# The third half projection of the next head, moved in front of the decay products

## The chip, the cores and the metric

The kernel runs on one core of a Trainium2 chip. The metric is the time of one execution on the device, in microseconds (us). A profiled execution is one further run, from which all rows of the trace below come; it has its own time.

## The reference, cut to what matters

All arithmetic is 32-bit floating point. The program is a chain of a gated delta-rule attention layer with 32 value heads, a perceptron, a second attention layer and a mixture of experts. The change lies in the first of these, with 1024 tokens of width 256:

```python
mixed = hidden_states @ w_qkv                      # 256 -> 2048 q, 2048 k, 4096 v
mixed = jax.nn.silu(_causal_conv(mixed, conv_w))   # 4 taps over the tokens
...
def step(state, xs):
    q_t, k_t, v_t, g_t, b_t = xs
    state = state * jnp.exp(g_t)[..., None, None]
    kv = jnp.einsum('bhk,bhkv->bhv', k_t, state)
    delta = (v_t - kv) * b_t[..., None]
    state = state + jnp.einsum('bhk,bhv->bhkv', k_t, delta)
    out = jnp.einsum('bhk,bhkv->bhv', q_t, state)
    return (state, out)
```

## The kernel before

The 16 key heads (each with two value heads) are worked one after the other, the tokens in 8 chunks of 128. The recurrence is replaced by a chunked form. A step h of the loop `STEPS` works on four heads at once: it projects the inputs of head h + 1 (`AHEAD`, steps 0 to 14), inverts the chunk matrices of head h (`INVERT`, steps 0 to 15), scans the state of head h - 1 through the chunks (`SCAN`, steps 1 to 16) and writes the output of head h - 2 (`FINISH`, steps 2 to 17).

Every engine runs through the same list of rows: `QUANTA` has 23 parts of the scan (chunk c, part 0, 1 or 2), and behind the part k an engine does what row k of `PLAN` names. A name stands for a group of products on PE and for what other engines do with their result. So `PLAN` is an order written out by hand, for PE, VectorE and ScalarE at once. The number beside a name is the PSUM bank, 0 to 3, into which the group is written. Per bank there are semaphores `full` and `free`, whose values are counted from the order in `PLAN`; a group waits until the one before it in its bank has been evacuated.

The names around the change:

- p0 to p7 (L531, `project`): the projections of the next head. Tensor j (key, query, two values) is made by p(2j) and p(2j+1), one half of the tokens each, as two products of 128x512 each, which are four instructions in the trace. They have no bank; they are written into the tile `pair` (two banks of its own). p2 belongs to tensor 1, so it may overwrite `pair` only when the last convolution tap of tensor 0 has read it (`conv_done`). Only the second half of a pair raises a semaphore (`pair_full`), and only on it ScalarE acts (L752, the last tap of the convolution). VectorE adds the other three taps (L900), at the rows in `TAPS`; tap 2 of tensor 0 stands in row 4.
- v0 to v2 (L653): transposes of the values, into banks 1 to 3. VectorE writes them to `v_s` (L990).
- decay0 to decay3 (L641, `decay0` issues all): 16 products of 2x128 by 2x128, 32 instructions, in four row groups of PE, into banks 3, 0, 1 and 2. All four banks must be free. VectorE bounds each bank from above (`Dm`, L999), which frees it, and ScalarE takes the exponential (L797).
- attn0 (L669) in row 7: products of keys and queries, into bank 1, which decay2 had. VectorE multiplies them by `Dm` (L1005).
- The scan between them: part 0 (L560, L562) reads the state S, VectorE makes X from it (L908); part 1 (L569) is called tx, VectorE copies it to Dl (L913), ScalarE scales it (L777); part 2 (L575, L579) gives outputs and the update of S (L921). Row 5 is part 0 of chunk 2, row 6 part 1 (tx2), row 7 part 2, row 8 part 0 of chunk 3.

GpSimd eliminates the blocks of head h + 1 (from L1105 on), SyncE carries them through memory into `Uf`, VectorE turns them to `Xh` (L960), and the group y6a (L675) of step h + 1 reads them.

Of the kernel before, what the change touches and what calls it, by code (L numbers as in the profile page):

```python
# [181 lines left out]
class Uses:  # L182
# [33 lines left out]
    [("z1", 3)],  # L216
    [("k0", 1), ("k1", 2)],
    [("v0", 1), ("v1", 2), ("v2", 3)],
    [("decay0", 3), ("decay1", 0), ("decay2", 1), ("decay3", 2), ("p2", None)],
    [("attn0", 1), ("p3", None)],  # L220
    [("flip0", 0)],
    [("kk0", 1), ("kk1", 3), ("v3", 2)],
# [1798 lines left out]
```

## Time and profile before

| | us |
|---|---|
| median of 3 runs | 1626.75 (1622.11 to 1628.88) |
| the profiled execution | 1633.12 |
| its span, first to last instruction | 1631.3 |
| steps 0 to 15 of the heads, decay products to decay products | 65.34 to 1061.73 |
| PE busy | 1418.5 (87% of the span) |
| VectorE busy | 1014.2 (62%) |
| ScalarE busy | 767.1 (47%) |
| GpSimd busy | 698.5 (43%) |

The groups of rows below are copied from the profile. PE is TensorE, DVE is VectorE, ACT is ScalarE, POOL is GpSimd. A row of the order in time gives start, duration (from the first start to the last end of a group), engine, line, operation, tiles, shape and count; in brackets stands how long the engine idled before it and what ended that.

### The profile page before, as it was taken

The page shows a single profiled execution, that of the slowest core. Times are in us where ns is not written, and L with a number is a line of the kernel's source. Part 1 is how long each engine was busy: PE and PEld are TensorE (multiplying, and loading weights), DVE is VectorE, ACT ScalarE, POOL GpSimd, SP SyncE. Part 2 cuts the span into 40 slices and gives each one's busy share as a digit, 9 for nine tenths or more (in the row PEclk, how much of TensorE's full clock was granted, in tenths as well). Part 3 has the DMA queues.
Part 4 walks back from the last instruction along what each step waited for, and adds up shares of the span by engine and source line. Part 5 has one row for each costly group of instructions (what it writes and reads, how often), then busy time and mean ns, then how long its engine had stood idle before and what let it go on. Part 6 is the DMA issues. An engine that isn't in the chain of part 4 may idle for free. (4 is left out here: it accounts for less than half of the span.)

```text
span 1631.3 us, 26379 instructions
## 1 busy us (share of the span) xinstructions
PE 1418.5 (87%) x9528; PEld 1000.0 (61%) x9528; DVE 1014.2 (62%) x2096; ACT 767.1 (47%) x1798; POOL 698.5 (43%) x1217
## 2 busy tenths in 40 slices
PE   6479899999999999999999999988597899688884
PEld 3246676777767777667676676776445466435552
DVE  5558777778777777777768777764303465621443
ACT  3336556565565655656656556654120464110110
POOL 1763763745637547365473663801100000061443
PEclk9779999999999999999999999999798999698997
DMA  3111111111111111111111111100161610121666
GB/s 84 42 32 37 27 39 35 40 37 20 43 30 40 38 24 41 31 39 37 24 42 35 33 37 37 23 12 7 59 285 33 136 40 1 58 88 50 128 135 146
DMA packets 127090, 86.72 MB, mean 53 GB/s; under 512 B 92339, under 2 KB 113031, under 8 KB 126193
## 3 DMA queue, kind: packets, MB, share of 16 engines
q1 hardware_dynamic: 120816, 76.50, 17.3%
q0 software_dynamic: 6144, 8.53, 3.0%
q8 instruction: 77, 1.26, 0.3%
q14 instruction: 53, 0.43, 0.1%
HBM read 61.65 MB, written 23.76 MB: 52 GB/s over the span
## 5 line engine op out<-in xcount | busy, mean ns | idle before, releaser
L531 PE MATMUL psum_banks<-main_hT,gdn_w_in 128*128 128x512 f32 x512 | 259.9, 634 | 20.5 <-DVE heads_y L900 18.3
L900 DVE SCALAR_TENSOR_TENSOR heads_y<-psum_banks,gdn_conv_w,heads_y 128x1021 f32<-128x1021 f32 (+2 forms) x192 | 245.3, 1278 | 44.0 <-ACT heads_y L752 42.1
L1115 POOL TENSOR_TENSOR heads_XT<-heads_XT,heads_tmp 128x126 f32<-128x126 f32 (+22 forms) x496 | 197.4, 398 | 38.8
L1112 POOL TENSOR_TENSOR heads_tmp<-heads_XT,heads_A 128x126 f32<-128x126 f32 (+22 forms) x496 | 192.2, 387 | 38.9
L531 PEld LDWEIGHTS psum_banks<-main_hT,gdn_w_in 128*128 128x128 f32 x512 | 94.1, 196 | 106.1 <-issue 87.2
L1097 POOL TENSOR_TENSOR heads_og<-heads_og,heads_fac 128x512 f32<-128x512 f32 x64 | 64.5, 1040 | 180.6 <-DVE heads_fac L971 180.6
L663 PE MATMUL psum_banks<-heads_w_o,heads_ogT 128*128 128x256 f32 x512 | 120.7, 385 | 3.6 <-ACT heads_ogT L818 3.6
L1105 POOL TENSOR_TENSOR heads_A<-heads_A,heads_cb 128x1024 f32<-128x1024 f32 x16 | 37.9, 2371 | 199.6 <-DVE heads_nd_t L953 183.0
L632 PE MATMUL psum_banks<-heads_w_z,main_hT 128*128 128x256 f32 x512 | 123.0, 383 | 0.0
L752 ACT ACTIVATE heads_y<-psum_banks,gdn_conv_w 128x1024 f32<-128x1024 f32 x64 | 71.3, 1113 | 105.3 <-PE psum_banks L531 104.9
L770 ACT ACTIVATE heads_O<-psum_banks,heads_coef 128x128 f32<-128x128 f32 x224 | 69.5, 362 | 91.5 <-PE psum_banks L562 90.3
L1708 POOL DMA_INDIRECT expert_rows<-moe_rows,route_dest x32 | 31.4, 981 | 189.2 <-issue 189.2
L777 ACT ACTIVATE heads_Dt<-heads_Dl,heads_coef 128x128 f32<-128x128 f32 x224 | 77.4, 394 | 65.3 <-DVE heads_Dl L913 65.3
L663 PEld LDWEIGHTS psum_banks<-heads_w_o,heads_ogT 128*128 128x128 f32 x512 | 94.8, 192 | 20.4 <-issue 9.1
L913 DVE COPY heads_Dl<-psum_banks 128x256 f32<-128x256 f32 x128 | 53.6, 419 | 75.9 <-PE psum_banks L569 75.9
L632 PEld LDWEIGHTS psum_banks<-heads_w_z,main_hT 128*128 128x128 f32 x512 | 92.8, 191 | 11.1
L788 ACT ACTIVATE heads_junk<-heads_og 128x128 f32<-128x128 f32 x256 | 78.1, 305 | 33.8 <-DVE heads_og L939 29.4
L908 DVE SCALAR_TENSOR_TENSOR heads_X<-psum_banks,heads_coef,heads_v_s 128x128 f32<-128x128 f32 x224 | 67.7, 343 | 39.4 <-PE psum_banks L560 39.4
L921 DVE SCALAR_TENSOR_TENSOR heads_S<-heads_S,heads_coef,psum_banks 128x128 f32<-128x128 f32 x192 | 57.8, 342 | 54.9 <-PE psum_banks L579 54.8
L575 PE MATMUL psum_banks<-heads_Dl,heads_At 128*128 128x128 f32 x512 | 87.2, 295 | 3.9 <-DVE heads_Dl L913 3.9
L569 PE MATMUL psum_banks<-heads_X,heads_Uf 128*128 128x128 f32 x448 | 74.5, 289 | 17.7 <-DVE heads_X L908 17.7
L575 PEld LDWEIGHTS psum_banks<-heads_Dl,heads_At 128*128 128x128 f32 x512 | 76.2, 201 | 21.3 <-issue 10.7
(252 smaller groups left out, 3067.3 us busy)
## 6 DMA issues: line engine op xcount, KB each, us to landing
main_w_gu<-in_w_gu SPq DMA_DIRECT2D x4, 2816.0 KB, 24.8
gdn_w_in<-in_w_in SPq DMA_DIRECT2D x16, 512.0 KB, 5.1
heads_A<-kk_blocks SPq DMA_DIRECT2D x64, 128.0 KB, 2.6
moe_wd<-in_w_down SPq DMA_DIRECT2D x32, 176.0 KB
expert_rows<-attn_zeros SPq DMA_DIRECT2D x1, 4624.0 KB, 25.9
moe_be<-expert_rows SPq DMA_DIRECT2D x32, 144.5 KB
heads_w_z<-in_w_z SPq DMA_DIRECT2D x16, 256.0 KB
heads_w_o<-in_w_o SPq DMA_DIRECT2D x16, 256.0 KB
```

The lines of the kernel that those rows point to most:

```text
L531: ins = pe.matmul(out[:, half * 512:(half + 1) * 512], w_in[:, kd_, j * P:(j + 1) * P], hT[:, kd_, half * 512:(half + 1) * 512], start=kd_ ...
L569: ins = pe.matmul(bank_a[:, e], Uf[old][:, e * C + c], rhs, start=True, stop=True)
L575: ins = pe.matmul(bank_b[:, e], At[old][:, c * HD + e], Dl[:, e], start=True, stop=True)
L632: ins = pe.matmul(flat(bank[b][:, 2 * j:2 * j + 2]), hT[:, k, c * P:(c + 1) * P], w_z[:, k], start=k == 0, stop=k == KD - 1)
L663: ins = pe.matmul(flat(bank[b][:, 2 * j:2 * j + 2]), ogT[:, c * HD + e], w_o[:, e], start=e == 0, stop=e == HD - 1)
L752: act.activation(y[j][:], out, ACT.Copy, scale=conv_w[:, head, j, 3:4]).then_inc(pair_base.sem, 1)
L770: ins = act.activation(O1[:, e], bank_b[:, e], ACT.Copy, scale=coef[:, GAM, h - 1, i:i + 1])
L777: ins = act.activation(Dt[:, e], Dl[:, e], ACT.Copy, scale=coef[:, TAIL, h - 1, i:i + 1])
L788: act.activation(junk[:], og[(h - 1) % 2][:, c * HD + e], ACT.Square, accum_out=ms[:, c * HD + e:c * HD + e + 1]).then_inc(sq_ready.sem, 1)
L900: dve.scalar_tensor_tensor(y[j][:, shift:T], src[:, 0:T - shift], conv_w[:, head, j, t:t + 1], y[j][:, shift:T], ALU.mult, ALU.add).then_i ...
L1112: pool.tensor_tensor(tmp[:, 0:n, 0:m], bc_last(XT[:, 0:n, j], m), bc_mid(A0[:, j, j + 1:BLK], n), ALU.mult).then_inc(solve_step.sem, 1)
L1115: pool.tensor_tensor(XT[:, 0:n, j + 1:BLK], XT[:, 0:n, j + 1:BLK], tmp[:, 0:n, 0:m], ALU.add).then_inc(solve_step.sem, 1)
```

## The change

In row 6 of `PLAN` the entry p2 goes from the end of the row to its head. Nothing else of the program is changed. The order in the other rows, the banks, and all counts of semaphores stay the same, since p2 has no bank and raises nothing. In step 15 and later there is no p2.

```diff
     [("k0", 1), ("k1", 2)],
     [("v0", 1), ("v1", 2), ("v2", 3)],
-    [("decay0", 3), ("decay1", 0), ("decay2", 1), ("decay3", 2), ("p2", None)],
+    [("p2", None), ("decay0", 3), ("decay1", 0), ("decay2", 1), ("decay3", 2)],
     [("attn0", 1), ("p3", None)],
     [("flip0", 0)],
```

## Rows read from the trace of the kernel before

**Rows 1.** The page, PE's busy time and PE's granted clock in 40 slices.
```profile
PE 1418.5 (87%) x9528; PEld 1000.0 (61%) x9528; DVE 1014.2 (62%) x2096; ACT 767.1 (47%) x1798; POOL 698.5 (43%) x1217
...
PEclk9779999999999999999999999999798999698997
```

**Rows 2.** Stretches: length; busy PE, PEld, DVE, ACT, POOL; clock; DMA share, GB/s.
```profile
261.18:328.79 67.61, 64.30 (x490) 47.85 (x491) 50.74 (x102) 40.31 (x98) 38.14 (x71) 0.97 0.15 35
...
396.41:462.36 65.95, 62.63 (x490) 47.03 (x491) 50.73 (x102) 40.31 (x98) 38.15 (x71) 1.00 0.15 35
462.36:529.99 67.63, 64.31 (x491) 48.02 (x491) 50.78 (x102) 40.30 (x98) 38.16 (x71) 0.97 0.14 34
...
1400.00:1631.00 231.00, 176.26 (x640) 107.52 (x640) 86.50 (x251) 29.76 (x81) 80.71 (x64) 0.88 0.44 105
```

**Rows 3.** Waits of PE: line, whom it waited for, us in total, times, longest.
```profile
PE psum_banks L641 <- DVE heads_v_s L990: 18.2, 16, 1.2
...
PE psum_banks L675 <- DVE heads_Xh L960: 12.0, 2, 11.3
```

**Rows 4.** Stretches around decay products of step 6, and ahead of step 5's.
```profile
461.00:464.37 3.37, 2.20 (x36) 1.50 (x35) 2.39 (x6) 3.03 (x10) 0.00 (x0) 1.00 0.00 0
464.37:467.78 3.41, 3.41 (x9) 2.17 (x8) 1.64 (x3) 3.09 (x9) 0.00 (x0) 0.50 0.00 0
...
392.69:396.10 3.41, 1.93 (x15) 1.38 (x13) 3.41 (x7) 2.02 (x7) 0.00 (x0) 1.00 0.00 0
396.10:399.50 3.40, 3.09 (x38) 2.04 (x39) 2.42 (x6) 3.08 (x6) 0.00 (x0) 1.00 0.00 0
```

**Rows 5.** Order in time, PE, step 6: the decay products and attn0.
```profile
462.36 1.18 PE L641 MATMUL psum_banks<-heads_row_to,heads_row_from 2*128 2x128 f32 x32 [1.17 <-DVE heads_v_s L990]
...
467.84 1.05 PE L669 MATMUL psum_banks<-heads_qT,heads_kT 128*128 128x128 f32 x8
```

**Rows 6.** Order in time, PE, step 7: tx2 to part 0 of chunk 3.
```profile
528.10 0.71 PE L569 MATMUL psum_banks<-heads_X,heads_Uf 128*128 128x128 f32 x4 [0.61 <-DVE heads_X L908]
529.99 1.17 PE L641 MATMUL psum_banks<-heads_row_to,heads_row_from 2*128 2x128 f32 x32 [1.17 <-DVE heads_v_s L990]
531.09 1.98 PE L531 MATMUL psum_banks<-main_hT,gdn_w_in 128*128 128x512 f32 x4
532.91 0.61 PE L575 MATMUL psum_banks<-heads_Dl,heads_At 128*128 128x128 f32 x4
...
533.79 1.05 PE L669 MATMUL psum_banks<-heads_qT,heads_kT 128*128 128x128 f32 x8
...
536.40 0.59 PE L560 MATMUL psum_banks<-heads_S,heads_kT 128*128 128x256 f32 x2
```

**Rows 7.** Order in time, DVE, step 7.
```profile
526.26 1.27 DVE L900 SCALAR_TENSOR_TENSOR heads_y<-psum_banks,gdn_conv_w,heads_y 128x1023 f32<-128x1023 f32 x1
...
527.97 1.88 DVE L990 TENSOR_TENSOR heads_v_s<-psum_banks,heads_k_root 128x512 f32<-128x512 f32 x3
...
531.15 2.48 DVE L999 TENSOR_TENSOR heads_Dm<-psum_banks,heads_limit 128x512 f32<-128x512 f32 x4 [0.98 <-PE psum_banks L641]
533.99 0.60 DVE L921 SCALAR_TENSOR_TENSOR heads_S<-heads_S,heads_coef,psum_banks 128x128 f32<-128x128 f32 x2 [0.36 <-PE psum_banks L579]
...
535.40 1.41 DVE L1005 TENSOR_TENSOR heads_At<-psum_banks,heads_Dm 128x256 f32<-128x256 f32 x4
537.03 0.61 DVE L908 SCALAR_TENSOR_TENSOR heads_X<-psum_banks,heads_coef,heads_v_s 128x128 f32<-128x128 f32 x2 [0.23 <-PE psum_banks L560]
```

**Rows 8.** Order in time, PE, step 15, which has no p2.
```profile
1061.73 1.17 PE L641 MATMUL psum_banks<-heads_row_to,heads_row_from 2*128 2x128 f32 x32 [0.86 <-DVE heads_v_s L990]
...
1064.84 1.86 PE L669 MATMUL psum_banks<-heads_qT,heads_kT 128*128 128x128 f32 x8 [0.85 <-DVE heads_Dm L999]
```

**Rows 9.** Order in time, ACT, step 7: the four exponentials.
```profile
532.21 2.19 ACT L797 ACTIVATE heads_Dm<-heads_Dm 128x512 f32<-128x512 f32 x4
```

**Rows 10.** The page's costliest groups: GpSimd's first big operation of a step.
```profile
L1105 POOL TENSOR_TENSOR heads_A<-heads_A,heads_cb 128x1024 f32<-128x1024 f32 x16 | 37.9, 2371 | 199.6 <-DVE heads_nd_t L953 183.0
```

## The prediction

> **What bounds the kernel now.** I read the page first. PE is busy for 87% of the span and its granted clock stands at nine tenths or full almost everywhere [rows 1]. The table of busy time by step then splits the stage of the heads, where the change lies: step 5 has PE busy for 62.63 of 65.95 us while VectorE and ScalarE have 15 us and more to spare [rows 2]. So PE bounds these steps, and a step gets shorter only where PE idles or runs slowly. The list of waits shows where it idles: ahead of the decay products (L641) it stood 18.2 us in 16 waits for the third copy of `v_s` by VectorE [rows 3]. That is the place that the change touches.
>
> The same table shows a second thing. Full steps come in two lengths: 65.95 us at a granted clock of 1.00 (step 5) and 67.6 us at 0.97 (steps 3 and 6) [rows 2]. Steps 3, 4, 6, 8, 9, 11, 12 and 14 are at 0.97, which makes eight; steps 2, 5, 7, 10 and 13 are at 1.00. The difference is 67.63 - 65.95 = 1.68 us. In step 6 it lies right behind the decay products. From 461.00 to 464.37 us PE was busy for 2.20 us of 3.37: it waited 1.17 us and then ran 32 products whose operands have two rows. From 464.37 to 467.78 us the clock was at 0.50 (1.2 GHz in place of 2.4) [rows 4]. In that step the score products (attn0) begin 467.84 - 462.36 = 5.48 us behind the decay products [rows 5]; in step 7, at full clock, 533.79 - 529.99 = 3.80 us behind [rows 6]. The difference is 1.68 us again: all of the longer step is this one fall.
>
> **The change part by part.** Nothing is removed or added. The four instructions of p2 (1.98 us when they follow the decay products, [rows 6]) go ahead of the 32 of decay0 in PE's queue in steps 0 to 14. p2 issues no DMA, raises no semaphore (only the second half of a pair does) and has no entry in the work of ScalarE, VectorE, GpSimd or SyncE, so those four queues keep their order. Step 15 has no p2 and stays as it is.
>
> The wait of p2. It overwrites half of the pair tile, so it waits for the last convolution tap of p0 and p1. That tap runs 526.26 to 527.53 us; PE comes free at 528.65 [rows 6, 7]. VectorE runs this tap ahead of the `v_s` copies, so p2 can never be ready later than the decay products. The wait costs nothing, with 1.1 us of cover in a full step; without that cover p2 would delay the decays by as much as the tap is late.
>
> The idle time ahead of the decays. The product before them ends at 528.81, and the next of PE's groups starts 0.16 us before the end that is shown (531.09 + 1.98 = 533.07 against a start at 532.91 [rows 6]). So p2 runs from 528.65 to 530.63, and the decays start at 530.47 in place of 529.99: the wait of 1.17 us is covered, and they are 0.48 us late.
>
> Where that gain goes. p2 also had a use where it stood: it hid the time in which VectorE empties the decay banks. attn0 writes bank 1, which decay2 has filled, and must wait for its evacuation. Step 15 shows the order without p2: decays at 1061.73, attn0 at 1064.84 after a wait of 0.85 us for the evacuation, 3.11 us behind [rows 8]. In a full step attn0 then starts at 530.47 + 3.11 = 533.58 in place of 533.79. Of 1.17 us, 0.21 is left, and a new wait of some 0.9 us stands ahead of attn0. VectorE allows about as much: the evacuations start at 530.47 + (531.15 - 529.99) = 531.63 and take 2.48 us, so the state update starts at about 534.03 in place of 533.99, for which VectorE gives up the 0.36 us that it idled there. It stays busy until 536.84, when X of the next chunk can start; that product's input is ready at 533.58 + (537.03 - 533.79) = 536.82. X starts at 536.84 in place of 537.03, 0.19 us earlier [rows 7]. ScalarE's exponentials start at 532.21, behind its table load, and the first evacuation, a quarter of these 2.48 us, would end at 532.3, so they slip by 0.1 us at the start and by half a microsecond at the end; their readers (the products with Dm, 535.40) come 1 us later [rows 7, 9]. I take 0.2 us a step. Steps 1 to 14 count: 14 x 0.2 = 2.8 us. Bounds: 0.3 us if the decays start right with p2's last column (4.2), and a loss of 0.1 if the evacuations lose 0.3 more (-1.4). Step 0 gives nothing, since PE later stands 11.3 us of it in the wait for `Xh`, at the end of a chain through GpSimd and DMA [rows 3]. That chain does not bound the other steps: GpSimd idled 183.0 us ahead of its first big operation of a step, waiting for VectorE [rows 10].
>
> The clock. In the eight steps the fall follows upon 1.17 us of idleness joined to the two-row products. Now a full-width projection of 1.98 us stands ahead of them, the idleness is gone, and 0.9 us of it comes back 1 us behind them, with two full-width groups between. The trace shows both neighbours. In step 15, idleness of 0.86 us, decays, two groups and 0.85 us of idleness were followed by half clock (the products of attn0 took 1.86 us, 1.05 at full clock) [rows 6, 8]. In step 7 the idleness of 1.17 us with decays and then 3 us of dense work brought no fall. The changed step has only one of the two idle stretches, so it is denser than either place. It can still fall where the decays and the new wait come together in an unlucky place. I take one fall among fourteen in place of eight: 7 x 1.68 = 11.8 us. Bounds: none (8 x 1.68 = 13.4) and one in each of the 14 steps (a loss of 6 x 1.68 = 10.1).
>
> A rule of the Trainium skill speaks against this term. "TensorE: Matmul & The Clock Gate", section "Why this matters for your kernels", names long idle gaps as what lowers the clock, and waits like this of 1.17 us would be too short for it. By that rule the change would bring 2.8 us alone. The rows do not agree: the clock fell in step 6 with no longer wait before it. The same page (Part 4) says that transposes do not count as work for the clock; by it the stretch ahead of p2, made largely of transposes, would go on causing falls. Here 3.41 us with PE busy for only 1.93, mostly transposes, passed at 1.00, and the 3.40 us after it too [rows 4], so the trace does not agree there either.
>
> The rest of the program has the same instructions. Its stretches meet the clock at other moments: the last 231 us ran at 0.88 [rows 2], and one fall more or less is 1.7 us. I allow 3 us either way.
>
> The sum: 2.8 + 11.8 = 14.6 us. The profiled execution took 1633.1 us (span 1631.3, 1.8 around it), so it would take 1618.5. It lies 6.4 us above the median of 1626.75; the same saving from the median gives 1612.2 us, 0.9% less.
>
> **The rivals.**
> Rival 1, the falls stay. The order brings only the 0.2 us, because the two-row products and the new wait together bring the clock down in about eight steps still. For it: step 15 [rows 8]. Against it: the changed stretch is denser than any that fell. Time: 1626.75 - 2.8 = 1624 us, chance 0.20. A second way to the same time is that waits of a microsecond have nothing to do with the clock and the falls come from something that the change does not move; it gets 0.04. The skill's page of above stands behind that second way.
> Rival 2, slower: the new wait ahead of attn0 takes the clock down in each step. Place: the wait for decay2's evacuation, 0.9 us, 2 us behind the decays' start. Price: 14 falls in place of 8, 10.1 us, less 2.8: 1634 us. It decides from 10 falls on (2 x 1.68 = 3.4 against 2.8). For it: step 15 fell with this very wait. Against it: there the first wait was still in place, and a dense 1.98 us now replaces it.
> Rival 3, the change does not do what it says: p2 itself waits, because the tap is late, and the decays move back by more. Against it are the 1.1 us of cover. With each decay late by another 0.5 us and all falls gone: -13.4 + 14 x 0.3 gives 1617.5 us.
>
> **How the numbers follow.** Forecast 0.66, rival 1 0.24, rival 2 0.05, rival 3 0.05. The predicted time is the forecast's, 1612 us. Its own range is 1605 (4.2 + 13.4 and 3 from elsewhere) to 1619 (five falls left). To leave out no more than 2 in 10 the range must take in rival 1: 1605 to 1625 us. A measurement of this kernel can tell about 0.5% (8.1 us) from no change; the borders are 1618.6 and 1634.9. Faster by more than that: forecast nearly whole and most of rival 3, 0.68. Within it: rival 1, most of rival 2 and the forecast's tail, 0.28. Slower: 0.04, the upper part of rival 2.
>
> **What would show it right or wrong.** In the list of waits, L641 should lose its 18.2 us but for step 15, and L669 should show a wait of 0.7 to 1.1 us for `heads_Dm` in each of 14 steps. In the table by step, steps 2 to 14 should be 65.7 to 65.8 us at 1.00, with one at about 67.4. The decays should follow p2 without idle time, and X of chunk 3 should start 0.2 us earlier against the tx2 group than in step 7. If the steps still alternate between two lengths, rival 1 holds; if all are at 0.97, rival 2; if L531 waits for a tap ahead of the decays, rival 3. The prediction is wrong if the idle time turns up elsewhere in the step, or if the falls have another cause than the stretch around the decays.

## The result, and the profile after

The changed kernel took 1614.95 us (median of 20 runs, 1608.01 to 1621.54), the kernel before 1623.37 us beside it (20 runs, 1616.72 to 1629.40). The ratio is 0.9944, with a 95% interval of 0.9928 to 0.9960: faster by 0.56%, or 8.4 us. Forecast were 14.6 us. The time lies in the range of 1605 to 1625 us and the direction is the forecast one; the gain is 0.58 of the one forecast.

The changed kernel's page, and its waits of PE (line, whom it waited for, us in total, times, longest), which answer to [rows 1, 3]:

```profile
PE 1413.1 (88%) x9528; PEld 993.8 (62%) x9528; DVE 1013.3 (63%) x2096; ACT 770.8 (48%) x1798; POOL 699.7 (43%) x1217
...
PEclk9879999999999999999999999999889899789998
```

```profile
PE psum_banks L669 <- DVE heads_Dm L999: 15.2, 16, 2.0
...
PE psum_banks L675 <- DVE heads_Xh L960: 11.0, 2, 10.3
...
PE psum_banks L641 <- DVE heads_v_s L990: 0.9, 1, 0.9
```

The 18.2 us ahead of the decay products are gone but for step 15. Ahead of attn0 (L669) there are now 15.2 us of waiting, where the kernel before had 0.9 us, in step 15 alone. In each of steps 1 to 14 it is 0.88 us, so of the 1.17 us that the move takes away three quarters come back ahead of the next group that needs one of these banks. The order in time on PE, in step 9 of the changed kernel (clock 1.00), against [rows 6], and on VectorE against [rows 7]:

```profile
661.58 0.71 PE L569 MATMUL psum_banks<-heads_X,heads_Uf 128*128 128x128 f32 x4 [0.61 <-DVE heads_X L908]
662.13 1.88 PE L531 MATMUL psum_banks<-main_hT,gdn_w_in 128*128 128x512 f32 x4
663.94 1.17 PE L641 MATMUL psum_banks<-heads_row_to,heads_row_from 2*128 2x128 f32 x32
665.05 0.71 PE L575 MATMUL psum_banks<-heads_Dl,heads_At 128*128 128x128 f32 x4
...
667.08 1.16 PE L669 MATMUL psum_banks<-heads_qT,heads_kT 128*128 128x128 f32 x8 [0.88 <-DVE heads_Dm L999]
...
669.79 0.59 PE L560 MATMUL psum_banks<-heads_S,heads_kT 128*128 128x256 f32 x2
```

```profile
665.13 2.48 DVE L999 TENSOR_TENSOR heads_Dm<-psum_banks,heads_limit 128x512 f32<-128x512 f32 x4 [1.48 <-PE psum_banks L641]
667.54 0.59 DVE L921 SCALAR_TENSOR_TENSOR heads_S<-heads_S,heads_coef,psum_banks 128x128 f32<-128x128 f32 x2
...
670.42 0.61 DVE L908 SCALAR_TENSOR_TENSOR heads_X<-psum_banks,heads_coef,heads_v_s 128x128 f32<-128x128 f32 x2
671.20 1.28 DVE L900 SCALAR_TENSOR_TENSOR heads_y<-psum_banks,gdn_conv_w,heads_y 128x1021 f32<-128x1021 f32 x1 [0.17 <-ACT heads_y L752]
```

The tap behind X, in step 7 of the kernel before, for later use:

```profile
537.81 1.28 DVE L900 SCALAR_TENSOR_TENSOR heads_y<-psum_banks,gdn_conv_w,heads_y 128x1021 f32<-128x1021 f32 x1 [0.16 <-ACT heads_y L752]
```

Counted from the start of tx2, the decays come at 2.36 us (1.89 before), attn0 at 5.50 (5.69), part 0 of chunk 3 at 8.21 (8.30), X of chunk 3 at 8.84 (8.93), the tap of the convolution behind it at 9.62 (9.71). So the direct gain is 0.09 us a step. The step table of the changed kernel (columns as in [rows 2]) shows it in the full steps, and shows the clock:

```profile
464.77:532.23 67.46, 64.43 (x492) 47.93 (x491) 50.61 (x101) 40.56 (x99) 38.36 (x71) 0.97 0.15 35
532.23:598.08 65.85, 62.82 (x491) 46.76 (x490) 50.73 (x101) 40.55 (x99) 38.19 (x71) 1.00 0.15 35
...
464.40:467.80 3.40, 2.62 (x40) 1.73 (x38) 1.92 (x5) 3.09 (x5) 0.00 (x0) 1.00 0.00 0
467.80:471.22 3.42, 3.31 (x10) 2.54 (x11) 3.21 (x11) 2.00 (x7) 1.30 (x2) 0.50 0.00 0
```

Steps at 1.00 take 65.85 to 65.90 us (65.93 to 65.95 before). Five steps of 1 to 14 (1, 2, 4, 6 and 11) still hold a fall to 0.50 behind the decay products, where eight did before. In step 6 it comes 3.0 us behind their start, just as attn0 begins after its wait; before, it came 2.0 us behind [rows 4, 5]. Steps with the same waits hold a fall or not (step 6 does and step 7 does not, in either kernel). So the waits and products decide whether the clock can fall there, and the moment at which they come whether it does.

How far the profiled pair misleads: its spans differ by 17.5 us. From the decays of step 1 to those of step 15 the kernel before takes 928.15 us and the changed one 922.87, 5.3 us less. Step 1 alone got 3.0 us longer (64.64 in place of 61.67), with a fall at its decays that it did not have before; steps 2 to 14 got 8.3 us shorter. The rest of the difference is mostly behind step 15, where neither the instructions nor the order differ. The stretch from there to the end, in the kernel before, in the same kernel profiled once more, and in the changed one:

```profile
1061.73:1700.00 638.27, 457.13 (x2232) 291.95 (x2232) 233.07 (x562) 156.59 (x356) 98.95 (x79) 0.92 0.28 75
```

```profile
1060.58:1700.00 639.42, 453.34 (x2232) 290.48 (x2232) 233.22 (x562) 156.76 (x356) 98.96 (x79) 0.92 0.27 75
```

```profile
1056.17:1700.00 643.83, 454.58 (x2232) 291.66 (x2232) 233.15 (x562) 156.51 (x356) 98.98 (x79) 0.92 0.27 74
```

The right ends are only set beyond the spans. With spans of 1631.3, 1617.7 and 1613.8 us the stretches are 569.6, 557.1 and 557.6 us long. The same kernel differs by 12.5 us from one execution to the next, in a part that the change does not reach. Of these, 7.4 us arise between the first products of L1594 and of L1619 and 4.2 us from there to those of L1799, all in the mixture of experts. So below I compare the stretch from step 1 to step 15, and ratios of many runs.

### The profile page after: what moved, and what is told of

The parts are those of the page before. It is cut to its first block and busy times, and to the rows that moved or that the text cites. A ratio compares the mean times of both kernels' runs of the same rounds, so it can differ in the third digit from the quotient of the medians.

```text
span 1613.8 us, 26379 instructions
## 1 busy us (share of the span) xinstructions
PE 1413.1 (88%) x9528; PEld 993.8 (62%) x9528; DVE 1013.3 (63%) x2096; ACT 770.8 (48%) x1798; POOL 699.7 (43%) x1217
## 5 line engine op out<-in xcount | busy, mean ns | idle before, releaser
L531 PE MATMUL psum_banks<-main_hT,gdn_w_in 128*128 128x512 f32 x512 | 254.8, 623 | 20.7 <-DVE heads_y L900 18.5
L900 DVE SCALAR_TENSOR_TENSOR heads_y<-psum_banks,gdn_conv_w,heads_y 128x1021 f32<-128x1021 f32 (+2 forms) x192 | 245.2, 1277 | 43.7 <-ACT heads_y L752 41.7
L908 DVE SCALAR_TENSOR_TENSOR heads_X<-psum_banks,heads_coef,heads_v_s 128x128 f32<-128x128 f32 x224 | 67.6, 342 | 43.8 <-PE psum_banks L560 42.9
L569 PEld LDWEIGHTS psum_banks<-heads_X,heads_Uf 128*128 128x128 f32 x448 | 61.4, 192 | 41.2 <-issue 21.5
L1788 POOL DMA_INDIRECT expert_sum<-moe_ys,moe_place x32 | 49.3, 1541 | 75.0 <-DVE moe_ys L1866 70.7
```

The lines of the kernel that those rows point to most:

```text
L531: ins = pe.matmul(out[:, half * 512:(half + 1) * 512], w_in[:, kd_, j * P:(j + 1) * P], hT[:, kd_, half * 512:(half + 1) * 512], start=kd_ ...
L569: ins = pe.matmul(bank_a[:, e], Uf[old][:, e * C + c], rhs, start=True, stop=True)
L900: dve.scalar_tensor_tensor(y[j][:, shift:T], src[:, 0:T - shift], conv_w[:, head, j, t:t + 1], y[j][:, shift:T], ALU.mult, ALU.add).then_i ...
```

## The experiments

The theory on the result: what the change brings is mainly that the clock falls less often, and the falls that are left come from the new wait ahead of attn0 next to the decay products. Against it stood that the waits do not matter for the clock, and that the decay products alone bring it down. All kernels in one table, times in us. "Falls" are falls of PE's clock to 0.50 around the decay products of steps 1 to 14, read from the step table (the step is at 0.97) and from narrower stretches; "full step" is one at 1.00. Not counted is a fall some 40 us behind the decay products of step 1, which stands in all of these kernels but p2_twice, thin3 and thin3_wide. Falls and lengths come from one profile of each kernel. Each ratio is that of many runs to the kernel before in the same comparison, and the comparisons did not all run on one chip: the kernel before took 1635.12 us beside p2_twice, split, bank_after and bank_before, 1636.73 beside after_again, p3_first, split_bank and thin3, 1625.24 beside before_again and the wide kernels, 1621.31 beside thin3_wide.

| kernel | wait ahead of decays, of attn0 | falls | full step | steps 1 to 15 | ratio to before |
|---|---|---|---|---|---|
| before | 1.17, 0 | 8 | 65.94 | 928.15 | 1 |
| changed | 0, 0.88 | 5 | 65.86 | 922.87 | 0.9944 (0.9928 to 0.9960) |
| before_again | 1.17, 0 | 8 | 65.94 | 928.19 | 0.9987 (0.9968 to 1.0007) |
| after_again | 0, 0.88 | 3 | 65.86 | 917.83 | 0.9907 (0.9872 to 0.9942) |
| p2_twice | 0, 0 | 0 | 66.42 | 920.79 | 0.9961 (0.9935 to 0.9987) |
| split | 0.31, about 0.15 | 0 | 65.36 | 907.90 | 0.9871 (0.9834 to 0.9909) |
| bank_after | 0, 0 | 0 | 65.42 | 907.18 | 0.9857 (0.9819 to 0.9895) |
| bank_before | 1.24, 0 | 8 | 66.02 | 929.24 | 1.0010 (0.9982 to 1.0038) |
| p3_first | 0, 0 | 0 | 65.42 | 906.94 | 0.9841 (0.9807 to 0.9874) |
| split_bank | 0.38, 0 | 0 | 65.16 | 903.88 | 0.9826 (0.9793 to 0.9859) |
| thin3 | 0, 0 | 12 | 67.22 | 943.29 | 1.0093 (1.0060 to 1.0126) |
| thin3_wide | 0, 0 | 0 | 67.19 | 931.66 | 1.0064 (1.0041 to 1.0087) |
| wide_before | 1.17, 0 | 9 | 65.94 to 66.09 | 930.93 | 1.0024 (1.0001 to 1.0046) |
| wide_after | 0, 0.88 | 0 | 65.86 | 912.93 | 0.9936 (0.9909 to 0.9964) |

**p2_twice: more work, and faster.**

```diff
-    [("p2", None), ("decay0", 3), ("decay1", 0), ("decay2", 1), ("decay3", 2)],
+    [("p2", None), ("decay0", 3), ("decay1", 0), ("decay2", 1), ("decay3", 2), ("p2", None)],
```

> The third half projection is computed twice, once ahead of the decay products and once more behind them (the second overwrites the first with the same values), so PE has 1.72 us more to do in each of 15 steps. Both waits, 1.17 us ahead of the decays and 0.88 us ahead of attn0, are covered. Theory 1 (falls of the clock come from idle time next to the decay products): no fall in steps 1 to 14, a full step of 65.94 + 1.72 - 1.17 = 66.5 us, and against before 14 x 0.55 - 8 x 1.68 = 5.7 us less in spite of 3% more work in the step, some 1617.5 us. Rival A (the clock has nothing to do with these waits): eight falls stay and the time is 7.7 us more than before, some 1631 us. Rival B (the two-row products alone bring it down): some falls stay, 3 to 5 of them, 1623 to 1626 us.

A step in the middle, and the whole of steps 1 to 14:

```profile
661.54:727.96 66.42, 64.27 (x495) 47.60 (x495) 50.72 (x101) 40.54 (x99) 38.16 (x71) 1.00 0.15 35
...
134.60:1055.39 920.79, 886.51 (x6857) 656.37 (x6857) 704.70 (x1406) 562.80 (x1366) 530.40 (x990) 1.00 0.15 35
```

The clock is at 1.00 throughout. Full steps are 0.48 us longer than before, yet the 14 steps together are 7.4 us shorter and the runs 0.39% faster (6 us; 5.7 were expected). PE computes half a projection for nothing in every step and gains by it. Rival A, which wanted 7.7 us more, is out: the waits, or the full-width work that fills them, have to do with the clock. Rival B is out too: the two-row products are all still there, and it wanted 3 to 5 falls.

**bank_after, bank_before and p3_first: only the new wait is taken away.** attn0 shares bank 1 with decay2, the third to be evacuated. The first two give that bank to decay0 (first hunk; bank_before has p2 at the end of the row), the third hides the wait behind p3 (second hunk).

```diff
-    [("p2", None), ("decay0", 3), ("decay1", 0), ("decay2", 1), ("decay3", 2)],
+    [("p2", None), ("decay0", 1), ("decay1", 0), ("decay2", 3), ("decay3", 2)],
...
-    [("attn0", 1), ("p3", None)],
+    [("p3", None), ("attn0", 1)],
```

> The changed kernel, with decay0 in bank 1 and decay2 in bank 3, so that attn0 (bank 1) waits for the first evacuation of the four and not for the third. The wait of 0.88 us ahead of attn0 should fall to nothing. VectorE has its work without a gap from the evacuations to X of chunk 3, so X should start at the same time as in the changed kernel, and about 1 us of idle time should turn up on PE ahead of tx3, 3 us further from the decay products; a full step stays at 65.85 us. Theory 1 (the falls left in the changed kernel come from this wait standing close to the decay products): the clock falls in 0 or 1 of steps 1 to 14 in place of 5, and the time is about 6 us under the changed kernel's, some 1609 us. Rival (the two-row products alone bring the clock down, or the wait hurts wherever it stands): 3 to 5 falls, the time of the changed kernel, 1615 us.

> The kernel before, with the same exchange of the banks of decay0 and decay2. attn0 did not wait there, and the wait of 1.17 us ahead of the decays stays. Theory 1 and the rivals agree: eight or so falls in steps 1 to 14, full steps of 65.94 us, the time of before within 0.3%. A gain here would show that the exchange helps by something else than the wait ahead of attn0.

> The changed kernel, with the fourth half projection (p3, 1.72 us of dense work) moved ahead of attn0 in the next row, so that it covers the wait for the evacuation of decay2 as p2 did in the kernel before. attn0 then ends at 4.9 us after the decays, just when VectorE comes free for it (4.99 us in the changed kernel). Theory 1: no idle time next to the decay products, no fall in steps 2 to 14, and the pair tile is full 1 us earlier, so that the tap of VectorE starts 6.8 us after the decays as with the exchanged banks: full steps of 65.4 us, 1.4% under before. Rival: attn0 is late for VectorE, X of chunk 3 slips by 0.2 to 0.5 us, full steps of 65.9 to 66.2 us, with no falls all the same: 0.8 to 1% under before.

PE in step 9 of bank_after:

```profile
652.15 0.71 PE L569 MATMUL psum_banks<-heads_X,heads_Uf 128*128 128x128 f32 x4 [0.61 <-DVE heads_X L908]
...
654.51 1.17 PE L641 MATMUL psum_banks<-heads_row_to,heads_row_from 2*128 2x128 f32 x32
...
656.60 1.05 PE L669 MATMUL psum_banks<-heads_qT,heads_kT 128*128 128x128 f32 x8
657.49 1.88 PE L531 MATMUL psum_banks<-main_hT,gdn_w_in 128*128 128x512 f32 x4
...
660.75 0.66 PE L657 MATMUL psum_banks<-main_ident,heads_og 128*128 128x128 f32 x4 [0.52 <-POOL heads_og L1097]
```

The same step on VectorE, X of chunk 3 and the tap:

```profile
660.83 0.60 DVE L908 SCALAR_TENSOR_TENSOR heads_X<-psum_banks,heads_coef,heads_v_s 128x128 f32<-128x128 f32 x2
661.34 1.27 DVE L900 SCALAR_TENSOR_TENSOR heads_y<-psum_banks,gdn_conv_w,heads_y 128x1021 f32<-128x1021 f32 x1
```

attn0 starts 2.09 us behind the decays in place of 3.14. No fall is left around the decay products, neither here nor in p3_first, which closes the same gap in another way. With the order of before the exchange of banks does nothing (8 falls, ratio 1.001), so it helps only where the wait ahead of attn0 is. The falls left in the changed kernel needed that wait, and the two-row products alone, which are still there, do not bring the clock down. Both edits also shorten the step, and a rival is that the length of the step sets how often a fall meets it. The table speaks against it: kernels without a fall have full steps of 65.16, 65.36, 65.42, 65.86, 66.42 and 67.19 us, those with falls 65.86, 65.94, 66.02 and 67.22. I was wrong on one point: full steps fell to 65.42 us where I expected 65.85. I had looked at X of chunk 3 only, which moved by 0.16 us. Behind it stands VectorE's tap of the convolution (L900), which in the changed kernel waits for ScalarE and so for p3. p3 comes 1.15 us earlier, that tap no longer waits, and it starts 6.83 us behind the decays in place of 7.26: 0.43 us, the length that the step lost.

**split and split_bank: the best of both places.** p2 is cut in two by its sum. `project` gets the range of the sum as an argument, and the row reads:

```diff
-    [("p2", None), ("decay0", 3), ("decay1", 0), ("decay2", 1), ("decay3", 2)],
+    [("pa2", None), ("decay0", 3), ("decay1", 0), ("decay2", 1), ("decay3", 2), ("pb2", None)],
```

> The third half projection is cut in two by its sum: its first product (two of the four instructions, 0.86 us) stays ahead of the decay products, its second goes behind them again. In the trace before, the wait ahead of the decays is 1.17 us and the changed kernel has one of 0.88 us ahead of attn0; this kernel should have 0.3 and 0.15. Theory 1 (the gain is the clock that no longer falls, the direct part is small because p2 is missed behind the decays): the decays start on time as before, attn0 0.6 us earlier than before, X of chunk 3 0.58 us earlier, a full step takes 65.4 us, and the clock falls in no step from 2 to 14. Against before: 14 x 0.58 + 8 x 1.68 = 21 us less, some 1602 us; against the changed kernel 12 to 13 us less. Rival (idle time is not what brings the clock down, the two-row products are): three to five falls of 1.68 us stay as in the changed kernel, some 1609 us.

> Both edits that helped, together: the third half projection cut in two around the decay products, and the banks of decay0 and decay2 exchanged. Cutting alone gave full steps of 65.36 us, in which VectorE starts the tap behind X of chunk 3 7.22 us after the decays, 0.16 us of it waiting for ScalarE; the exchange alone gave 65.42 us with that tap 6.83 us after the decays, since the fourth half projection comes earlier. If the two gains lie at different places, as the traces say, they add up: tx2 to decays 1.89 us and decays to tap 6.8 us, a full step of 64.9 to 65.0 us, no fall of the clock in steps 2 to 14, and 14 x 0.4 = 6 us less than cutting alone: 1.6% under before. Rival (another chain, of VectorE from the first tap on or of GpSimd's normalisation ahead of flip0, sets the length from here): full steps of 65.3 us, the same time as cutting alone.

Step 9 of split:

```profile
651.84 1.02 PE L531 MATMUL psum_banks<-main_hT,gdn_w_in 128*128 128x512 f32 x2
653.18 1.17 PE L641 MATMUL psum_banks<-heads_row_to,heads_row_from 2*128 2x128 f32 x32 [0.31 <-DVE heads_v_s L990]
654.28 1.13 PE L531 MATMUL psum_banks<-main_hT,gdn_w_in 128*128 128x512 f32 x2
...
656.28 1.16 PE L669 MATMUL psum_banks<-heads_qT,heads_kT 128*128 128x128 f32 x8
```

Half of p2 leaves a wait of 0.31 us ahead of the decays and almost none behind: attn0 starts 0.59 us after the group ahead of it, 0.44 us in bank_after where nothing waits. The decays start on time, the full step loses 0.58 us (65.94 to 65.36, as worked out ahead), and no fall stands around the decay products. Some 21 us less than before were expected, and the medians are 20.3 us apart (1614.79 against 1635.12). With both edits the gains add up in part only: 65.16 us in place of the 64.9 to 65.0 expected, since the tap then starts at 6.96 us behind the decays and the decays themselves 0.07 us later. split_bank is the fastest kernel of the study, 0.9826 of before and, in the same comparison, 1608.3 us against 1619.5 for the changed kernel.

**thin3: no idle time, and the clock falls.** Are the decay products themselves work or idleness for the clock? On top of bank_after they are issued three times over (the semaphores are raised by the last ones).

```diff
-                    for s in range(4):
+                    for n in range(12):
+                        s = n % 4
```

> The changed kernel with exchanged banks (in which the clock fell in no step from 2 to 14), with the 16 decay products issued three times over, with the same values: some 3 us of products with two rows in place of 1.17 us, and no idle time beside them. Each of 16 steps gets 1.8 us longer by the added instructions, 29 us in all. Theory 1a (these products are for the clock nearly as good as idleness, which is why a wait next to them brought it down): the clock falls behind them in about half of the steps though PE is never idle there, another 6 to 8 times 1.7 us, some 1651 us where the kernel with exchanged banks takes 1613. Theory 1b (a busy PE keeps its clock, only the waits counted): no falls, some 1641 us.

The stretch behind the decays' start in step 3 (268.13), and the next one:

```profile
268.60:272.01 3.41, 3.41 (x99) 3.20 (x92) 0.90 (x2) 1.45 (x2) 0.00 (x0) 1.00 0.03 5
272.01:275.42 3.41, 3.41 (x12) 2.38 (x12) 3.38 (x10) 2.94 (x8) 0.36 (x1) 0.50 0.01 2
```

PE is busy for 3.41 us of 3.41, and then runs at 1.2 GHz. That happened in 12 of the 14 steps. The full step grew by 1.80 us, as expected, and the kernel took 1652 us where theory 1a said 1651. That closeness is luck in part: it had 6 to 8 falls at 1.7 us, and there were 12 at 0.94 us (68.16 against 67.22 us). Theory 1b (no falls, 1641 us) is out. The rule of the Trainium skill ("TensorE: Matmul & The Clock Gate", section "Why this matters for your kernels") that idle gaps between bursts of matmuls lower the clock does not cover this: here the trace shows no gap.

**wide_before, wide_after and thin3_wide: the number of rows.** Each decay product spans 32 rows in place of 2, the added ones being zero in both operands; GpSimd writes these zeros once, at the start. Count, output and duration of the products stay (270 ns each by the trace).

```diff
-                            r, out = slice(32 * g, 32 * g + 2), bank[BANK[f"decay{g}"]]
+                            r, out = slice(32 * g, 32 * g + 32), bank[BANK[f"decay{g}"]]
```

> The kernel before, with the order of its row untouched, but each decay product spans 32 rows of its row group in place of 2 (30 of them are zero in both operands, so the sums are the same). The four groups together then use all 128 rows. Twelve to twenty small fills are added at the start, which the wait for Xh in step 0 should hide. The products take as long as before and the wait of 1.17 us ahead of them stays. Theory 2 (products on few rows are for the clock like idleness): with full products there only the wait is left, the clock falls in 0 to 2 of steps 1 to 14 in place of 8 or 9, and the time is 10 to 13 us (0.6 to 0.8%) under before without any change of order. Rival (the number of rows does not matter, the waits alone or short products do it): 8 or 9 falls, the time of before.

> The changed kernel with the decay products on 32 rows in place of 2. The wait of 0.88 us ahead of attn0 stays, full steps stay at 65.86 us. Theory 2: no falls in steps 1 to 14 in place of 3 to 5, and 5 to 8 us less than the changed kernel; against wide_before only the direct gain of the order is left, 0.08 us a step, 1 us in all. Rival: 3 to 5 falls, the time of the changed kernel.

> The kernel with the decay products issued three times over and exchanged banks, once more, but each product spans 32 rows in place of 2 (the added ones zero), as in the two wide kernels. Count, shape of the output and duration of the products stay. With two rows the clock fell in 12 of steps 1 to 14 though PE had no idle time beside them, and full steps took 68.2 us (67.2 where it did not fall). Theory 2 (few rows in use are what makes these products poor for the clock): no falls in steps 1 to 14, all steps 67.2 us, 12 x 0.94 = 11 us less than with two rows, so 0.3% over before in place of 0.9%. Rival (it is that they are short, or four at a time): 12 falls and the same time as with two rows. The kernel before gives the measure.

With two rows (thin3) most full steps were at 0.97 and 68.2 us; with 32 rows (thin3_wide) all are at 1.00 and 67.18 to 67.20 us, and steps 1 to 15 take 11.6 us less (11 expected). The wide version of the changed kernel has no fall at the decays either, with its wait of 0.88 us in place and full steps of the same 65.86 us. The whole of its steps 1 to 14, and step 1, which holds the one fall in them, 40 us behind the decays (in the mean of the whole it is rounded away):

```profile
136.00:1048.93 912.93, 867.39 (x6801) 646.02 (x6801) 703.88 (x1406) 563.18 (x1366) 532.59 (x990) 1.00 0.15 35
136.00:197.44 61.44, 56.18 (x444) 40.45 (x443) 48.62 (x96) 38.03 (x95) 34.41 (x67) 0.97 0.17 38
```

These steps are 9.9 and 4.9 us shorter than in the two profiles of the changed kernel. The runs do not show that gain: 5 to 8 us less than the changed kernel were expected, and the ratio of 0.9936 lies between the 0.9944 and the 0.9907 of the changed kernel, which was not run beside it.

So in the changed order and in thin3 it is the two rows that make the decay products bring the clock down. In the order of before the expectation failed: 9 falls, not 0 to 2, and no gain (1.0024). The falls had moved. In step 7, whose wide decays start at 534.64 us:

```profile
531.61:535.02 3.41, 1.62 (x21) 1.22 (x23) 3.22 (x7) 2.42 (x8) 0.00 (x0) 0.99 0.00 0
535.02:538.43 3.41, 3.41 (x34) 2.15 (x27) 2.01 (x4) 3.11 (x6) 0.00 (x0) 0.51 0.00 0
```

The clock now fell 0.4 us behind the start of the decays (0.0 to 1.0 us over the nine), not 1.6 to 2.5 us as in the kernel before. What stood ahead of that is the end of the `v` transposes, the wait of 0.61 us, tx2 and the wait of 1.17 us, with PE busy for 1.62 us of 3.41. In the order of before the two waits ahead of the decays are enough, with 32 rows in the products. In the changed order neither is enough alone: the wait of 0.88 us brings falls only beside two-row products (wide_after has none), and the two-row products, issued once, only beside the wait (bank_after has none).

**before_again and after_again: how steady is the count?**

> The kernel before itself, profiled on this chip as the measure for the two others. 8 or 9 falls of the clock behind decay products in steps 1 to 14, full steps of 65.94 us, a ratio of 1.000 within 0.3%.

> The changed kernel itself, as the measure for the others on the same chip. 0.56% under before as in its first comparison, with 3 to 6 falls of the clock in steps 1 to 14 and full steps of 65.86 us. Had its profile caught a lucky or unlucky execution, the number of falls would be outside that.

The kernel before had 8 falls both times, in other steps (3, 5, 6, 8, 9, 11, 13, 14 the second time). The changed kernel had 5 and 3. The second comparison gave 0.9907 where the first gave 0.9944; their intervals overlap a little. Three to five falls fewer at 1.68 us and 1.1 us of direct gain make 6 to 10 us, or 0.4 to 0.6%, and the second profiled pair has 10.4 us in steps 1 to 15. The 15 us of the second comparison are more than that. Each run's mean granted clock, over the whole program, is on record too. For the changed kernel it is 0.952 in the first comparison and 0.953 in the second. For the kernel before it is 0.944 in the second, and 0.946 and 0.947 in the two comparisons on other chips. So in the second comparison it was the kernel before that spent more time at the lower clock. Where in the program, these runs do not settle; the part behind step 15 alone varies by 12 us.

## Why the prediction was right, and where it was off

- **The number**: nearer than the gain, by luck. 1612.2 us lie 2.8 us from the 1614.95 measured, though the gain was 6.2 us too large. The forecast was counted from a median of 3 runs, 1626.75, which lies 3.4 us above that of 20. Counted from there, the measured gain gives 1618.3 us, at the upper end (1619, five falls left) of the forecast's own range. The lower end was mis-added: 1626.75 less 4.2, 13.4 and 3 is 1606, not 1605.
- **The wait that goes**: right. PE's 18.2 us ahead of L641 are 0.9 us, in step 15.
- **What bounds the steps**: in part. A step gets shorter where PE stands idle less, but the row that sets its length is the tap behind X, which X of chunk 3 only stood in for. Behind tx2 it starts at 9.71 us before, 9.62 in the changed kernel, 9.19 in bank_after, and full steps are 65.94, 65.86 and 65.42 us. X starts at 8.93, 8.84 and 8.68. In the changed kernel both moved alike, so the forecast did not suffer by it.
- **The new wait ahead of attn0**: right. It was put at about 0.9 us, from step 15, and is 0.88 us in each full step. Its place is the third evacuation, as bank_after shows by moving it to the first.
- **The start of the decays and of attn0**: right within 0.03 us (2.37 and 5.48 us behind tx2 forecast, 2.36 and 5.50 measured).
- **The direct gain**: 0.2 us forecast, 0.08 measured. The term that failed is the distance from attn0 to X of chunk 3, taken over from the kernel before; in it stand 2.61 us from attn0 to part 0. There attn0 followed other products without a gap. Behind a wait its group takes 1.16 us in place of 1.05, and the 2.61 are 2.71. p3, on which the tap hangs, starts later by the same 0.1 us. Over 14 steps this is 1.1 us in place of 2.8.
- **The clock**: the mechanism was right and its size was not. Eight falls were to become one; they became five and, in the second profile, three. The step that failed is "it is denser than either place". I compared how much idle time stood around the decays and did not count the decays themselves. thin3 shows that such products bring the clock down without idle time, and the changed step has 1.17 us of them and 0.88 us of idle time with 1.1 us of full products between. Nor did I ask why 8 of 14 steps fell in the kernel before, when all 14 have the same waits; from the places alone no count can be worked out. wide_after shows the same from the other side: with full rows the same wait brings no fall. With four falls left, the mean of the two profiles, the sum would have been 1.1 + 4 x 1.68 = 7.8 us, against 8.4 measured; with the five of the first it is 6.1.
- **The rest of the program**: 3 us either way was too little for one execution. It is 12 us between two profiles of the same kernel. The median of 20 runs made up for it.
- **The rivals**: rival 2 (a fall in every step) and rival 3 (p2 waits itself) are out. p2 started without a wait. Rival 1 (eight falls stay) is out in its size, but its cause, step 15's pattern, is what is left in three to five steps. Its second way, that waits of a microsecond have nothing to do with the clock, is refuted by bank_after, with p2_twice beside it.

## What to carry to other kernels

When a group of products is moved forward to fill a wait, ask what it was hiding where it stood; half of it may be enough in each place, and the bank that the next group wants may be freed first instead of third. In a kernel bound by TensorE, look at the granted clock next to each short wait: here the wait was 1.17 us long, and the fall behind it cost 1.68 us more in eight of 14 steps; closing both gaps was worth two to three times the move alone (0.9826 against 0.9907 in the same comparison, 0.9944 in the first). When you look for the cause of a fall, suspect not only idle time but also products on few rows.

## What the runs showed of the hardware that was not expected

- The clock fell to 1.2 GHz with PE busy for the whole of the 3.41 us before (thin3), and did not when the same instructions used 32 rows in place of 2 (thin3_wide): 12 falls against 0.
- The falls come in a rhythm. In the kernel before, steps of 67.6 us with a fall and of 65.9 us without take turns, one or two of the longer behind each of the shorter, so that 8 of 14 fall, in both profiles and with exchanged banks too, though in different steps. A kernel on the border (the changed one) has a count that varies from run to run, 5 and 3. That is why one profile says little about what is left.
- A fall costs 1.68 us in the kernel before [rows 2] but 0.94 us in thin3 (68.16 against 67.22 us). Why it is less there was not looked into.
